# Two cross-attention layers on one core: row sums from a split sum of the weights, ahead of the weighted sums

## The reference

```python
# layer 0
Q, K, V = x @ Wq + bq, ctx @ Wk + bk, ctx @ Wv + bv
x = x + softmax(Q @ K.T / sqrt(512), axis=-1) @ V @ Wo + bo
# layer 1: the softmax runs over the 256 rows of x (axis=1), not over the keys
q, k, v = x @ Wq1 + bq1, ctx @ Wk1 + bk1, ctx @ Wv1 + bv1
w = softmax(q @ k.T / sqrt(512), axis=1)
y = w @ v + x
out = (y - mean(y)) * rsqrt(var(y) + 1e-6) * gamma + beta
```

## Time and profile before

| | |
|---|---|
| time, median of 3 runs | 1176.57 us (1173.44 to 1177.16) |
| the profiled execution, its own time | 1174.09 us |
| its span in the trace | 1172.3 us |
| PE busy | 1147.3 us, 98% of the span |
| DVE, ACT, POOL busy | 899.4, 855.1 and 961.2 us (77%, 73% and 82%) |
| mean of the 16 DMA engines' busy share over most of the span | about 0.65 |
| granted clock of PE, mean | 0.997 |

### The profile page before, as it was taken

One profiled execution on the slowest core, in us unless ns is written; L12 is line 12 of the kernel. 1 busy time (PEld: TensorE's weight loads), 2 busy tenths in 40 slices (PEclk: granted clock), 3 DMA queues, 4 the chain that ended last, 5 costly groups with the idle time before them and its releaser, 6 DMA issues.

```text
span 1172.3 us, 25323 instructions
## 1 busy us (share of the span) xinstructions
PE 1147.3 (98%) x8001; PEld 1070.1 (91%) x8001; DVE 899.4 (77%) x2081; ACT 855.1 (73%) x1733; POOL 961.2 (82%) x767
## 2 busy tenths in 40 slices
PE   9989999999999999999999999999999999999985
PEld 7879999999999999999999999999999999999974
DVE  2667787787777778778778778777777877877887
ACT  2557777777777777777777777777777778777763
POOL 2458898898898888889889889889888888988864
PEclk9999999999999999999999999999999999999998
DMA  8455666666666666666667666666666666666631
GB/s 337 165 189 200 216 223 221 213 233 204 223 230 206 225 230 211 217 221 218 221 212 222 219 214 235 201 224 238 196 227 226 215 218 218 222 221 213 196 105 75
DMA packets 131551, 249.04 MB, mean 212 GB/s; under 512 B 15680, under 2 KB 88896, under 8 KB 123072
## 3 DMA queue, kind: packets, MB, share of 16 engines
q1 hardware_dynamic: 130512, 247.59, 62.7%
q10 hardware_dynamic: 1008, 1.06, 0.3%
HBM read 165.16 MB, written 83.43 MB: 212 GB/s over the span
## 4 chain that ended last, share of the span: by engine, by line
PE 94%; DVE 2%; ACT 1%; issue 1%; DMA 1%; POOL 1%; SPq 0%; POOLq 0%; DVEq 0%; ACTq 0%
PE bank L366 90%; PE bank L444 2%; PE bank L506 1%; PE bank L513 1%; PE bank L533 1%; DMA PT_raw<-E_dram 0%; SPq L255 0%; DVE R L981 0%; ACT bank L760 0%; DMA gT<-g_dram 0%; POOLq L69 0%; DVE y_blk L989 0%; POOL Y L1397 0%; ACT Y L788 0%; DVE w_lo L1032 0%
## 5 line engine op out<-in xcount | busy, mean ns | idle before, releaser
L1336 POOL TENSOR_TENSOR xT_lo<-IN,xT_hi 128x1024 fp32r<-128x1024 f32 x64 | 154.5, 2414 | 21.0 <-ACT xT_hi L652 21.0
L1336 POOL TENSOR_TENSOR yT_lo<-yT_raw,yT_hi 128x1024 fp32r<-128x1024 f32 x63 | 149.9, 2380 | 18.6 <-ACT yT_hi L652 17.3
L1397 POOL TENSOR_TENSOR Y<-Y,gamma_b 128x512 f32<-128x512 f32 x126 | 160.5, 1297 | 3.0 <-ACT Y L788 3.0
L1400 POOL TENSOR_TENSOR Y<-Y,beta_b 128x512 f32<-128x512 f32 x126 | 161.2, 1302 | 0.0
L788 ACT ACTIVATE Y<-R,nmr,rstd 128x512 f32<-128x512 f32 x126 | 96.0, 810 | 74.6 <-POOL nmr L1384 74.6
L366 PE MATMUL bank<-yT_hi,A_hi 128*128 128x256 f32 x512 | 144.6, 282 | 1.1 <-issue 1.1
L366 PE MATMUL bank<-xT_hi,A_hi 128*128 128x256 f32 x512 | 144.6, 282 | 1.1 <-DVE A_lo L1124 1.1
L1382 POOL TENSOR_TENSOR rstd<-ve,half 128x2 f32<-128x2 f32 x63 | 44.5, 707 | 123.3 <-DVE nmu L1080 123.3
L366 PE MATMUL bank<-xT_hi,A_lo 128*128 128x256 f32 x512 | 144.6, 282 | 0.0
L366 PE MATMUL bank<-yT_lo,A_hi 128*128 128x256 f32 x512 | 144.4, 282 | 0.0
L366 PE MATMUL bank<-xT_lo,A_hi 128*128 128x256 f32 x512 | 144.2, 282 | 0.0
(11 more groups left out here) (130 smaller groups left out, 4242.1 us busy)
## 6 DMA issues: line engine op xcount, KB each, us to landing
IN<-in_packed SPq DMA_DIRECT2D x64, 1024.0 KB, 5.0
R<-in_x SPq DMA_DIRECT2D x64, 512.0 KB, 4.3
y_dram<-y_blk SPq DMA_DIRECT2D x252, 128.0 KB, 2.5
yT_raw<-y_dram SPq DMA_DIRECT2D x63, 512.0 KB, 3.5
out<-Y SPq DMA_DIRECT2D x63, 512.0 KB, 2.6
E_dram<-E_blk SPq DMA_DIRECT2D x256, 64.0 KB, 1.7
PT_raw<-E_dram SPq DMA_DIRECT2D x64, 256.0 KB, 2.7
gT<-g_dram SPq DMA_DIRECT2D x64, 128.0 KB, 3.8
```

Of the source, the lines that this page charges most:

```text
L1336: return nc.gpsimd.tensor_tensor(dst, src, fp(hi), ALU.subtract)
L1397: nc.gpsimd.tensor_tensor(y[:, q, :], y[:, q, :], gamma_b[:, :], ALU.mult).then_inc(Y_mul, 1)
L1400: last = nc.gpsimd.tensor_tensor(y[:, q, :], y[:, q, :], beta_b[:, :], ALU.add)
```

## The change

`w_los` and its sum go. In their place, per sequence: ACT's `w_1_` writes half 1 of the weights in plain float32 (`w_1`), DVE's `w_sum_` adds half 0 to it (`w_sum`, 128 x 256), ACT's `w_sums_h` and POOL's `w_sums_l` split that sum into a hi and a lo tile, and PE's `s_` needs two matmuls instead of three. PE does `s_` ahead of `wc_` instead of behind it. Some calls change places in the other engines' orders.

```diff
 PE   s_(n):
-                pe.wait_ge(w_los_set, n.count())
-                for t, part in enumerate((w[0][:, 0, :], w[0][:, 1, :], w_los[:, :])):
-                    last = nc.tensor.matmul(s_bank[:, 0:S], ones[:, :], part, start=(t == 0), stop=(t == 2))
+                pe.wait_ge(w_sums_lo, n.count())
+                for t, part in enumerate(w_sums):
+                    last = nc.tensor.matmul(s_bank[:, 0:S], ones[:, :], part[:, :], start=(t == 0), stop=(t == 1))
 PE   body:
                 v_(r.plus(1))
+                s_(r)
                 wc_(r)
-                s_(r)
 ACT
+            def w_1_(n):
+                act.wait_ge(rz1_set, n.count())
+                first(act, w_sum_set, n.count(back=1))
+                copy(w_1[:, :], S1_bank[:, S:2 * S], scale=rz1[:, 1:2]).then_inc(w_1_set, 1)
+            def w_sums_h(n):
+                act.wait_ge(w_sum_set, n.count())
+                first(act, s_full, n.count(back=1))
+                copy(w_sums[0][:, :], w_sum[:, :]).then_inc(w_sums_hi, 1)
 ACT  body:
                     PT_h(r.plus(2))
-                    u_h(r.plus(3))
                     C_h(r.plus(3))
                 xT_h(r.plus(4))
                 if prefix:
+                    u_h(r.plus(3))
                     out_seed_(r.plus(2))
...
                 exps0(r.plus(3))
+                cT_h(r.plus(4))
+                w_1_(r)
                 w_h(r)
-                cT_h(r.plus(4))
+                w_sums_h(r)
                 normalise(r.plus(-1))
 DVE
+            def w_sum_(n):
+                dve.wait_ge(w_1_set, n.count())
+                dve.wait_ge(w_hi, n.count())
+                first(dve, w_sums_lo, n.count(back=1))
+                nc.vector.scalar_tensor_tensor(w_sum[:, :], S1_bank[:, 0:S], rz1[:, 0:1], w_1[:, :], ALU.mult, ALU.add
+                                               ).then_inc(w_sum_set, 1)
 DVE  body:
+                x2(r.plus(-1), 0)
                 g_blocks(r.plus(1))
-                x2(r.plus(-1), 0)
...
                 rz1_(r)
+                E0_blocks(r.plus(3))
                 stats_ready(r.plus(-1))
-                E0_blocks(r.plus(3))
+                x1(r.plus(2), 0)
                 variances(r.plus(-1))
-                x1(r.plus(2), 0)
+                w_sum_(r)
+                x1(r.plus(2), 1)
                 w_l(r)
-                x1(r.plus(2), 1)
                 y_blocks(r.plus(2))
+                s_columns(r)
                 v_l(r.plus(1))
-                s_columns(r)
 POOL
+            def w_sums_l(n):
+                pool.wait_ge(w_sums_hi, n.count())
+                minus(w_sums[1][:, :], w_sum[:, :], w_sums[0][:, :]).then_inc(w_sums_lo, 1)
 POOL body:
                 yT_l(r.plus(1))
+                cT_l(r.plus(4))
                 scales(r.plus(-1))
-                cT_l(r.plus(4))
-                w_low_sum(r)
+                w_sums_l(r)
```

More of the change, by code:

```diff
@@ L122, in build @@
         gT = sb("gT", [P, 1, S])
-        w_los = sb("w_los", [P, S], f32r)
+        w_1 = sb("w_1", [P, S])
+        w_sum = sb("w_sum", [P, S])
+        w_sums = split("w_sums", [P, S])
         scol = sb("scol", [P, ST, 32])
@@ L176, in build @@
         S1_seed, S1_full, nmax1_set, E1_set = sem("S1_seed"), sem("S1_full"), sem("nmax1_set"), sem("E1_set")
-        rz1_set, w_hi, w_lo, w_los_set = sem("rz1_set"), sem("w_hi"), sem("w_lo"), sem("w_los_set")
+        rz1_set, w_hi, w_lo = sem("rz1_set"), sem("w_hi"), sem("w_lo")
+        w_1_set, w_sum_set = sem("w_1_set"), sem("w_sum_set")
+        w_sums_hi, w_sums_lo = sem("w_sums_hi"), sem("w_sums_lo")
         s_full, s_set = sem("s_full"), sem("s_set")
@@ L773, in w_h @@
                 last.then_inc(w_hi, 1)
+            def w_1_(n):
+                if not n.there():
+                    return
+                act.wait_ge(rz1_set, n.count())
+                first(act, w_sum_set, n.count(back=1))
+                copy(w_1[:, :], S1_bank[:, S:2 * S], scale=rz1[:, 1:2]).then_inc(w_1_set, 1)
+            def w_sums_h(n):
+                if not n.there():
+                    return
+                act.wait_ge(w_sum_set, n.count())
+                first(act, s_full, n.count(back=1))
+                copy(w_sums[0][:, :], w_sum[:, :]).then_inc(w_sums_hi, 1)
             def wc_h(n):
@@ L906, in _ @@
             exps0(T(3))
+            w_1_(T(0))
             w_h(T(0))
+            w_sums_h(T(0))
             normalise(T(-1))
@@ L914, in _ @@
             exps1(T(1))
+            w_1_(T(1))
             w_h(T(1))
+            w_sums_h(T(1))
             out_seed_(T(3))
@@ L925, in _ @@
             exps1(T(2))
+            w_1_(T(2))
             w_h(T(2))
+            w_sums_h(T(2))
             S1_seed_(T(3))
@@ L1277, in _ @@
             E0_blocks(T(3))
+            w_sum_(T(0))
             w_l(T(0))
@@ L1291, in _ @@
             x2(T(0), 1)
+            w_sum_(T(1))
             w_l(T(1))
@@ L1307, in _ @@
             rz1_(T(2))
+            w_sum_(T(2))
             w_l(T(2))
@@ L1367, in yT_l @@
                 minus(blocks(yT[1]), raw(yT_raw), blocks(yT[0])).then_inc(yT_lo, 1)
-            def w_low_sum(n):
+            def w_sums_l(n):
                 if not n.there():
                     return
[L1372 to L1375, removed]
+                pool.wait_ge(w_sums_hi, n.count())
+                minus(w_sums[1][:, :], w_sum[:, :], w_sums[0][:, :]).then_inc(w_sums_lo, 1)
             def scales(n):
@@ L1449, in _ @@
             scales(T(-1))
-            w_low_sum(T(0))
+            w_sums_l(T(0))
             finish(T(-1))
             PT_l(T(3))
-            w_low_sum(T(1))
+            w_sums_l(T(1))
             yT_l(T(2))
@@ L1456, in _ @@
             finish(T(0))
-            w_low_sum(T(2))
+            w_sums_l(T(2))
             scales(T(1))
```

## The result

| | before | after |
|---|---|---|
| median of the runs, us | 1175.65 (4 runs, 1173.44 to 1177.16) | 1186.39 (4 runs, 1185.68 to 1188.25) |
| ratio after / before | | 1.0102 (1.0088 to 1.0116) |
| profiled execution, own time, us | 1174.09 | 1186.91 |
| its span, us | 1172.3 | 1185.1 |
| mean step, from `max0` to `max0` over 57 steps, us | 17.360 | 17.523 |

The changed kernel is 1.0% slower, 10.7 us on the medians; 1190 was forecast, for a before of 1176.57. The two profiled executions lie 12.8 us apart: 9.3 between the first and the last step's `max0`, 2.1 in the end, and 1.4 in the start.

What follows compares the result with a forecast made beforehand. PE, 98% busy, was taken as the bound. A stall of 0.34 less 0.12 saved gives 0.22 us a step, 13.2 over 60 steps; with 0.8 for the end, +14.0, said as 1190 us, range 1178 to 1201.

Steps and rivals of the forecast that it cites:

- The stall: At PE's `s_`, now ahead of `wc_`: waits for POOL's `w_sums_l`, 0.34 us each step, ends 0.22 and 0.61.
- the 0.06 for unseen waits: On DVE: waits of `x1(0)` and `w_sum_` not shown by the trace, 0.06 us together, each bounded by 0 and 0.09.
- The lock: On DVE: `ve` is held until POOL's running `cT_lo` ends; 0.10 us more per step, left out of the sum, 10%.
- The third rival: DVE's `ve` waits for POOL's `cT_lo` and only then begins: 0.10 us more per step, 6 us, 1196; 10%.
- The links in between: From DVE's `w_sum_` (0.48 us) through ACT's `w_sums_h` (0.43) to POOL's `w_sums_l` (0.75), which starts once `scales` frees POOL.
- `w_lo` as a second limit: On DVE behind `w_sum_` and `x1(1)`: `w_lo` would start `wc_` at 617.29, 0.14 us late, hidden behind the 0.28.
- The second rival: Only `w_lo` is late at `wc_`, by 0.14 us, the sum's path being quicker: about +2 us, 1178; 8%.
- the first: Rival at `s_`: the sum is in time, PE never waits and all 7.5 us are gained, 1169; 12%.
- What the profile would show: PE idle about 0.3 us before `s_`, released by `w_sums_lo`; period about 17.6 us; none before `wc_`; clock 1.00.
- What moves at no price: Other reordered calls, such as `s_columns`, `g_blocks`, `u_h`, `y_blocks`: results 0.3 to 1.4 us later, covered, priced at zero.
- The end: T(0) to T(2), chains through ACT and DVE: about 0.7 us for one bare chain, +0.8 together, 1.5 either way.
- The matmul: At PE's `s_`: one matmul less saves 0.119 us per sequence, 7.1 us in the steady part, 7.5 in all.

Runs made afterwards that it cites:

- Experiment 4: The kernel before with only `s_` moved ahead of `wc_` in the 60 steps: 1221.43 us in a single run, step 18.179.
- experiment 2: The changed kernel with POOL doing `cT_l` behind `scales` and `w_sums_l` in the 60 steps: 1190.52 us, ratio to before 1.0134.
- experiment 3: The changed kernel with DVE's `stats_ready`, `E0_blocks` and `variances` ahead of `x1(0)`, `cT_l` still early on POOL: 1220.51 us in a single run.
- experiment 1: The changed kernel with `s_` back behind `wc_` in the 60 steps: 1187.05 us, ratio to before 1.0102.
- experiment 9: The changed kernel with the written-out end of the kernel before (`w_low_sum`, three matmuls for T(0) to T(2)), steps untouched: 1183.44 us, ratio to before 1.008.
- experiment 7: The kernel before with `s_` cut to two matmuls on `w_hi`, low part of the sum left out of the result: 1168.32 us, ratio 0.9949.
- experiment 6: The changed kernel with the old orders on all engines, only the sum computed the new way; in the end `w_l` ahead of `w_sum_`: 1173.4 us, ratio 0.9989.
- experiment 5: The changed kernel with `s_` behind `wc_` and DVE's `w_l` ahead of `w_sum_` and `x1(1)` in the 60 steps: 1170.83 us, ratio to before 0.9967.
- experiment 8: Kernel of experiment 5 with the written-out end of the kernel before (`w_low_sum`, three matmuls for T(0) to T(2)): 1168.67 us, ratio to before 0.9961.

## Why the prediction was right

- **The frame held.** PE sets the time, a step is worth its matmuls plus its waits, and a wait after `S0_` comes back in each step: the period grew by 0.163 us, which is 9 to 10 us for the 60 steps. With the 2.1 of the end that is 11.4 to 12; the medians differ by 10.7 and the two profiled executions by 12.8, and the rest lies in the start and in the spread of single runs. Experiment 4 shows that nothing is made up.
- **The stall: 0.28 measured (0.23 of it standing still), 0.34 forecast, 0.28 from the rows alone.** The step that was mis-sized is the 0.06 for unseen waits, which came out at nothing. But the agreement of the rest is luck: three errors cancel. The sum came sooner: `x1(0)` started 2.46 after `max0`, not 2.63, since it follows 0.04 after the *start* of `rz0` and not after its end, and since `rz0` was 0.05 earlier. The lock took most of that back: `ve` lasted 0.29 instead of 0.17, ending 0.03 after `cT_lo`. With these, `w_sum_` started at 3.65, against 3.73, and `w_sums_lo` ended at 5.48, against 5.56. And PE took 0.23 us from there to the first matmul that counts (605.58 to 605.81), not the 0.15 of the earlier trace rows: 5.48 + 0.23 and 5.56 + 0.15 are both 5.71. That `w_sums_lo` ended just at the moment when PE came by (605.58) and still cost 0.23 shows how much hung on this term.
- **The third rival was not a rival but a term.** I gave the lock 10% and left it out, because `ve` released at POOL's end would be done by 615.17 and hence before 615.21. That held only for an `x1(0)` as late as I had it. With `x1(0)` 0.17 sooner, `ve` ran into `cT_lo` in all four bodies of the loop, though in one of them by only 0.03 us (it took 0.20 there). Experiment 2 prices it at 0.12 us in the step shown and 0.10 on the mean, and experiment 3 shows its size when the meeting is longer. The Trainium skill, "SBUF — State Buffer", section "Who interferes with whom", says that the pair of ports is held for a whole instruction and that the other engine blocks fully; it lists `tensor_scalar`, which `ve` is, among the operations that can take it. The rows of experiment 3 agree, 0.89 against 0.17 us.
- **The links in between were right.** `w_sum_` took 0.47 (0.48 forecast), `w_sums_h` 0.42 (0.43), `w_sums_l` 0.74 (0.75). ACT's half was done at 604.67, but POOL was held by `scales` until 604.84, as forecast: POOL's queue and not the sum's own path set the start. One reading was loose: the prediction says that `w_sum_` doesn't wait for `w_hi`, while its code has that wait. It cost nothing, since `w_hi` was complete at 602.62 + 0.84 = 603.46, 0.29 us before `w_sum_` started.
- **`w_lo` as a second limit was there,** less late than I made it: it lets `wc_` start 5.72 after `max0` (experiment 1), where the forecast had 617.29 - 611.48 = 5.81, and PE without the stall would ask at 5.67. That is 0.05 late instead of 0.14, hidden behind the 0.28; experiment 1, where PE asks at 5.43, shows it bare. The second rival (only `w_lo` late) fell, since the sum was late as well; the first fell too, since nothing was in time.
- **What the profile would show.** The period came to 17.52 and not 17.6, the clock stayed at 1.00, and there was no wait ahead of `wc_`. The idle time "released by POOL's `w_sums_lo`" did not show on PE at all: 0.17 on the weight load, put down to issue, and the matmul of 0.36 us were its only direct traces. I had asked the profile for a line that it can't give for a wait this short.
- **What moves at no price** was priced rightly: after shows no other wait of PE in the steady part, though it doesn't price the 0.05 of slower pace in `out_` and `v_`. `cT_l`'s new place turned out to matter beyond the lock, and it was on the good side: experiment 2, which puts it behind the sum, where it stands in neither kernel, shows the bill at `PT_lo`.
- **The end: +2.1 measured, +0.8 forecast,** inside of the bound given. I let one of the three chains lie bare; by the waits of experiment 9 all three did: 0.95 behind T(0)'s weights, 0.68 and 0.64 at T(1)'s, 0.45 behind T(2)'s, part of it given back.
- **The matmul: 0.107 to 0.119,** with experiment 7 on the low side. By it the 7.1 us on offer in the steps would have been 6.4.

What stays open: why a released `s_` took 0.22 to 0.23 us to count (here and in experiments 2 to 4) where `wc_` and `Pc_` took 0.15 to 0.16. The difference lies ahead of the weight load, which starts 0.12 after the release here (605.58 to 605.70) and 0.05 after it in experiment 1 (608.18 to 608.23); from there to the first matmul that counts it is 0.11 in both. Open as well are the slower pace in `out_` and `v_` and what makes the end longer.

## What to carry to other kernels

Where one engine is the bound and works through a fixed order, an edit that moves a consumer ahead is paid by the slack of every producer on the way: write down for each the moment of supply and of demand, and move the consumer only as far as the smallest margin, less what a release takes. Separate "less work" from "new order" before trying both; here the lighter work in the old orders was 0.1% faster (experiment 6), in orders fitted to it 0.3% (experiment 5) and with the old end too 0.4% (experiment 8), while the orders that came with it made it 1.0% slower. A busy share of 100% doesn't exclude a stall: count the instructions in a fixed window, or take the period.

## What the runs showed of the hardware

- A tiny VectorE operation can last as long as GpSimd's current one. `tensor_scalar` on 128 x 2 in SBUF took 0.29 us in after, 0.89 in experiment 3 and 2.32 in the earlier trace rows, against 0.17 with GpSimd idle (62 times in before), and ended within 0.03 us of GpSimd's end each time. The two aggregations ahead of it ran beside the same `cT_lo` at 0.24 us (0.23 in the earlier trace rows), and `w_sum_`, with one operand in PSUM, beside `rstd` at its 0.47.
- A short wait of the matrix engine is written into a matmul's duration (0.36 instead of 0.28 us) rather than into idle time. A longer one, which outlasts the record of the matmul ahead of it, leaves idle time with its releaser: 0.55 and 0.52 us of the 0.78 lost in the steps of experiments 3 and 4, and down to 0.20 in the end of experiment 9.
- The matrix engine needs a result before the place of the matmul that reads it: ready 0.11 us ahead of that place it still cost 0.11 us (experiment 2). From the end of the result to the first matmul that counts it took 0.22 us at `s_` in all steps of after and experiments 2 to 4, and 0.16 at `wc_` in experiment 1; the weight load stands 0.11 before that matmul in both.
- On VectorE an instruction that needs the result of a 0.12 us `reciprocal` starts 0.04 us after the reciprocal's start, as the records have it, and not after its end (`x1(0)` behind `rz0` in after); one that doesn't need it starts after the same 0.04.
